# Half passes of q side by side in the two row halves of TensorE, with other first and last stages, in a two-layer decoder kernel

## What is computed

```python
x = _layernorm(x + _L0_attn_ref(x, ...))         # latent attention, 32 heads, causal, rotary
x = _layernorm(x + _L0_xattn_ref(ctx_512, x, ...))  # graph learned from the context, top 30% of a row
x = _layernorm(x + _L0_ffn_ref(x, ...))          # 7 routed experts (best 2) and a shared one
x = _layernorm(x + _L1_attn_ref(x, ...))         # attention, 16 heads, causal, rotary
x = _layernorm(x + _L1_xattn_ref(x, ctx_512, ...))  # bilinear softmax with the context
x = _layernorm(x + _L1_ffn_ref(x, ...))          # gated, 1024 wide
```

## Time and profile before

| | us |
|---|---|
| median of 3 runs | 673.74 (673.16 to 674.34) |
| the profiled execution's own time | 674.2 |
| its span | 672.3 |
| TensorE busy (PE) | 651.7, 97% |
| VectorE busy (DVE) | 524.2, 78% |
| ScalarE busy (ACT) | 502.5, 75% |
| GpSimd busy (POOL) | 389.5, 58% |

### The profile page before, as it was taken

The page is one execution under the profiler, slowest core; times in us unless marked ns, Lnnn a source line. Parts: engine busy times, 40 slices in busy tenths (PEclk is TensorE's granted clock), DMA queues, the critical chain, the costliest instruction groups (busy, mean ns, idle before and its releaser), DMA issues.

```text
span 672.3 us, 15731 instructions
## 1 busy us (share of the span) xinstructions
PE 651.7 (97%) x5342; PEld 557.9 (83%) x5342; DVE 524.2 (78%) x1684; ACT 502.5 (75%) x1305; POOL 389.5 (58%) x646
## 2 busy tenths in 40 slices
PE   8899999999999999999999999999989999999996
PEld 5589988989888899889877888889878887778885
DVE  2799988996999799767889945557798878858455
ACT  4799778878688885898887866665658786876544
POOL 3388658457664845698769455545872321445543
PEclk9999999999999999999999999999999999999998
DMA  8763022214213211310032012111020000011201
GB/s 259 188 186 86 18 71 59 77 26 118 49 56 103 49 50 47 95 33 2 1 96 63 1 54 87 48 49 47 1 95 5 3 3 4 3 48 48 94 1 63
DMA packets 35048, 40.17 MB, mean 60 GB/s; under 512 B 7052, under 2 KB 27798, under 8 KB 34968
## 3 DMA queue, kind: packets, MB, share of 16 engines
q1 hardware_dynamic: 34424, 38.84, 19.8%
q10 hardware_dynamic: 544, 0.33, 0.2%
HBM read 29.05 MB, written 1.05 MB: 45 GB/s over the span
## 4 chain that ended last, share of the span: by engine, by line
PE 82%; DVE 7%; ACT 4%; SPq 2%; issue 2%; DMA 1%; POOL 1%; DVEq 0%; POOLq 0%; ACTq 0%
PE bank L1242 72%; PE bank L1256 8%; SPq L2762 1%; PE bank L1542 1%; ACT probs L1922 1%; DMA xT_plain<-in_xT 1%; POOL qT L2487 1%; DVE bn L2034 1%; DMA qT<-xT_plain 1%; DVE ctx_pair_lo L2011 1%; DVE y L2011 1%; DVE probs L2162 1%; DVE g_pair_lo L2011 0%; ACT x L1684 0%; ACT xT_hi L1677 0%
## 5 line engine op out<-in xcount | busy, mean ns | idle before, releaser
L2484 POOL TENSOR_SCALAR probs<-probs,soft 128x256 f32<-128x256 f32 (+1 forms) x256 | 104.9, 432 | 52.1 <-DVE soft L2170 51.0
L1784 ACT ACTIVATE probs<-probs,soft 128x256 f32<-128x256 f32 (+1 forms) x256 | 113.2, 448 | 12.0 <-DVE soft L2162 11.1
L2487 POOL TENSOR_TENSOR w_split_lo<-w_raw,w_split_hi 128x512 fp32r<-128x512 f32 (+2 forms) x57 | 74.3, 1311 | 67.9 <-ACT w_split_hi L1677 67.7
L1242 PE MATMUL bank<-xT_hi,w_split_hi 128*128 128x512 f32 x256 | 103.8, 405 | 3.7 <-DVE xT_lo L2014 2.5
L1242 PE MATMUL bank<-xT_lo,w_split_hi 128*128 128x512 f32 x256 | 100.5, 393 | 0.0
L1242 PE MATMUL bank<-keyT,qT 128*64 128x192 f32 (+3 forms) x1024 | 80.4, 302 | 1.3 <-POOL qT L2487 1.3
L1242 PEld LDWEIGHTS bank<-keyT,qT 128*64 128x64 f32 x1024 | 74.2, 137 | 8.9 <-issue 3.6
L1242 PE MATMUL bank<-xT_hi,w_split_lo 128*128 128x512 f32 x192 | 75.5, 393 | 0.0
L2487 POOL TENSOR_TENSOR qT<-qT,xT_plain 64x512 f32<-64x512 f32 x44 | 56.5, 1283 | 31.8 <-DMA qT<-xT_plain 29.7
L2162 DVE CUSTOM_DVE_ANT_0 probs<-bank,mask 128x128 f32<-128x128 f32 (+1 forms) x192 | 58.0, 330 | 17.2 <-PE bank L1242 16.2
L1677 ACT ACTIVATE probsT<-bank 128x384 f32<-128x384 f32 x128 | 53.6, 494 | 13.9 <-PE bank L1256 13.4
(11 more groups left out here) (259 smaller groups left out, 1820.6 us busy)
## 6 DMA issues: line engine op xcount, KB each, us to landing
qT<-xT_plain SPq DMA_DIRECT2D x88, 64.0 KB, 2.0
w_raw_heads<-in_w_o SPq DMA_DIRECT2D x8, 512.0 KB, 4.6
w_raw<-in_w_nopeT SPq DMA_DIRECT2D x8, 384.0 KB, 3.1
qT<-rope_buf SPq DMA_DIRECT2D x40, 64.0 KB, 2.0
...
```

The costliest lines, as they stand in the source:

```text
L1242: return t.matmul(out, lhsT, rhs, start=start, stop=stop, skip_group_check=shared)
L1784: ins = s.activation(p[:, at], p[:, at], ACT.Exp, bias=st[:, 0, r:r + 1], scale=-1.0, accum_out=st[:, 1, r:r + 1])
L2484: return g_.tensor_scalar(out, in0, s1, s2, op0, op1)
L2487: return g_.tensor_tensor(out, in0, in1, op)
```

## The change

1. **q.** A step `q_full n g p` does the eight passes of 128 rows (for each kind the three of the first chunk and rest.hi x qaT.hi), and `q n g p` the two last passes, qaT.lo with the rest's high part, with 64 rows each. The rotary kind's high part stays in rows 0 to 63 and the latent kind's moves to rows 64 to 127 (`rest_rows`), so the two passes lie in different row halves and write two banks. qaT.lo has no zero rows any more. Both banks become ready with `q`; between `q_full` and `q` other steps may stand.
2. **First stage.** `down 1` follows `down 0`, keys are a step of their own (`key_T`, `key_scale`), adj_w, adj_qk, w_v 0 and adj_sim 0 stand ahead of the first q; w_v_latT and w_o of group 0 are loaded between xT0 and xT1, the inputs of w_k 0 behind xT1. ScalarE computes a square root of a constant at its start.
3. **Router.** Tokens are on the rows, the 8 + 8 columns are the high and low parts of the router's weights; VectorE adds the two parts and the bias. The copy and the transpose are gone.
4. **Experts.** u_pair.lo is formed from bank + bias - high part, and the bank is free after VectorE.
5. **out1.** Both bias passes first.
6. **Last stage.** `f_end i` keeps m = 7; m = 4 to 6 are `f_mid 0` (two tiles), `f_mid 1` and `f_mid 2` (one each). The last tile's store is issued by ScalarE.
7. **Order and costs.** A new PE_ORDER and ASIDE; Plan's cost of a shape change is stated per shape that is left (LEAVE) instead of 0.13 for all. `v1 0` moves ahead of `qkv 1 0` and of the first transposes of the second attention.

```diff
-            elif name == "q":
+            elif name == "q_full":
                 n, g, p = k
...
                 for kind in (1, 0):
                     out = wait_bank(("q", n, g, p, ("lat", "rot")[kind]))[:, :]
                     first, rest = (w_q[:, c, kind, 2 * p:2 * p + 2, :] for c in range(2))
-                    mm3(out, first, qaT[:, 0, at], True, False)
-                    mm(out, rest.hi, qaT.hi[:, 1, at], False, False)
-                    mm(out, rest.hi, qaT.lo[:, 1, at], False, True).then_inc(q_ready.sem, 1)
+                    mm3(out, first, qaT[:, 0, at], True, False, True)
+                    mm(out, rest.hi, qaT.hi[:, 1, at], False, False, True)
+            elif name == "q":
+                n, g, p = k
+                rest, at = group_q(g).hi[:, 1, :, 2 * p:2 * p + 2, :], slice(n * HALF, (n + 1) * HALF)
+                for kind in (1, 0):
+                    rows = rest_rows(kind)
+                    mm(bank_of(("q", n, g, p, ("lat", "rot")[kind]))[:, :], rest[rows, kind, :, :], qaT.lo[rows, 1, at],
+                       False, True, True).then_inc(q_ready.sem, 1)
...
+    def rest_rows(kind, low=False):
+
+        return slice(QREST, P) if (kind == 1) != low else slice(0, QREST)
...
-LOADS_AFTER = [("xT0", "xT1"), ("xT1", "xT2")] + [("xT2", name) for name in (
+LOADS_AFTER = [("xT0", "xT1"), ("xT1", 0), ("xT1", "xT2")] + [("xT2", name) for name in (
...
+                    w.wait_ge(*zeroed["unit"])
+                    s.activation(last_root[:, 0:1], plain(ones1[:, 0:1]), ACT.Sqrt)
...
-                terms = [(c, plain(part)) for c in range(DC) for part in (xT_pair.hi, xT_pair.lo)]
-                for n, (c, xt) in enumerate(terms):
-                    for i, tile in enumerate(tiles_of[h]):
-                        ins = mm(out[32 * i:32 * i + NE, 0:P], w_router[:, c, :], xt[:, c, tile * P:(tile + 1) * P],
-                                 n == 0, n == len(terms) - 1, True)
+                terms = [(part, c) for c in range(DC) for part in (xT_pair.hi, xT_pair.lo)]
+                for i, tile in enumerate(tiles_of[h]):
+                    for n, (part, c) in enumerate(terms):
+                        ins = mm(out[:, i * 2 * NE:(i + 1) * 2 * NE], part[:, c, tile * P:(tile + 1) * P],
+                                 w_router_parts[:, c, :, :], i == 0 and n == 0, n == len(terms) - 1, True)
...
-                    tt(up.lo[:, i, :], probs[in_probs.place["e_u", e, h, i]][:, :], plain(up.hi[:, i, :]),
-                       ALU.subtract).then_inc(e_u_lo.sem, 1)
+                    stt(up.lo[:, i, :], bank_of(("e_u", e, h, i))[:, :], b_up[:, e, i:i + 1], plain(up.hi[:, i, :]),
+                        ALU.add, ALU.subtract).then_inc(e_u_lo.sem, 1)
...
-            "e_u": lambda: e_u_copied[tuple(k)], "e_gate": lambda: e_silu[tuple(k)],
+            "e_u": lambda: e_u_lo[tuple(k)], "e_gate": lambda: e_silu[tuple(k)],
...
-f_up 1 7, f_end 0, f_end 1""")
+f_up 1 3, f_down 0 7, f_down 1 1, f_up 1 5, f_down 1 2, f_up 1 6, f_down 1 3, f_up 1 7, f_mid 0, f_mid 2, f_end 0,
+f_mid 1, f_end 1""")
...
+        b, i = LAST_STORED
+        w.wait_ge(*last_normed[b, i])
+        s.dma_start(out_dram[b, i * P:(i + 1) * P, :], x[:, TB * b + i, :]).then_inc(stored[b], 16)
```

More of the change, by code:

```diff
@@ L169 @@
 PE_ORDER = steps_of("""
-down 0, w_k 0, down 1, w_q 0, down_T 0, w_v 1, w_k 1, q 0 0 0, down_T 1, w_q 1, adj_w, w_v 0, adj_qk, q 0 0 1,
-q 1 0 0, s 0 0 0, s 1 0 0, q 1 0 1, adj_sim 0, s 0 0 1, s 1 0 1, q 1 1 0, pT 0 0 0, q 1 1 1, pT 0 0 1, pT 1 0 0,
-pT 1 0 1, s 2 0 0, pv 1 0, pv 0 0, s 2 0 1, w_k 2, s 3 0 1, s 3 0 0, q 0 1 0, out 1 0, pT 2 0 0, out 0 0, pT 2 0 1,
-s 2 1 1, pT 3 0 0, s 2 1 0, q 0 1 1, pT 3 0 1, pv 2 0, s 3 1 0, pv 3 0, s 3 1 1, out 2 0, out 3 0, pT 2 1 0,
-pT 3 1 0, pT 2 1 1, s 0 1 1, s 0 1 0, w_q 2, pT 3 1 1, pv 2 1, s 1 1 0, pv 3 1, s 1 1 1, q 1 2 0, q 1 2 1, pT 1 1 0,
@@ L431, in make_plan @@
         if n < U_EXPERT:
-            stage(("load", n, 0), "SP 2.6, DMA 2.5, WAY 2", *needs)
+            stage(("load", n, 0), "SP 2.6, DMA 2.5, WAY 2", *needs,
+                  *[By(("load", first), "SP") for first, then in LOADS_AFTER if n == then])
             stage(("load", n, 1), "SP 1.15, DMA 2.0, WAY 2", *[("w_v", n - 2)] if n >= 2 else [])
@@ L449, in make_plan @@
-        stage(("down_T", h), "PE 1.4, ACT 1.65, DVE 1.35", ("down_scale", h), ("down_rope", h), ("load", "identity"),
-              holds=[bank("qaT", h, c, left=(("down_T", h), "DVE")) for c in range(2)]
-              + [bank("keyT", h, left=(("down_T", h), "ACT"))], items=3)
-        stage(("key_swap", h), "SP 1.2, DMA 0.8, WAY 2", By(("down_T", h), "ACT"))
+        stage(("down_scale", h), "POOL 1.25, ACT 1.4", ("down_root", h), ("load", "const"), items=4)
+        stage(("key_scale", h), "DVE 0.95", ("down_root", h), ("load", "const"))
@@ L454, in make_plan @@
+        stage(("down_T", h), "PE 0.9, ACT 1.1, DVE 1.35", ("down_scale", h), ("load", "identity"),
+              holds=[bank("qaT", h, c, left=(("down_T", h), "DVE")) for c in range(2)], items=2)
+        stage(("key_T", h), "PE 0.45, ACT 0.55", ("key_scale", h), ("down_rope", h), ("load", "identity"),
+              holds=[bank("keyT", h, left=(("key_T", h), "ACT"))])
+        stage(("key_swap", h), "SP 1.2, DMA 0.8, WAY 2", By(("key_T", h), "ACT"))
     for g in range(NG):
         before = [] if g < 2 else [s for part in unit_readers(g - 2) for s in part]
-        stage(("w_k", g), "PE:cols64 0.7, ACT 0.85", ("load", g, 0),
+        stage(("w_k", g), "PE:cols64 0.65, ACT 0.65", ("load", g, 0),
@@ L538, in make_plan @@
         for h in range(NHALF):
-            stage(("e_u", e, h), "PE 2.79, ACT 2.5, DVE 1.3", ("split", U_EXPERT + e, 0), *[("xT", "experts", b) for b in halves(h)],
-                  *MOE_ROOM_LEFT, holds=[bank("e_u", e, h, i, left=(("e_u", e, h), "ACT")) for i in range(DC)]
+            stage(("e_u", e, h), "PE 2.79, ACT 2.5, DVE 1.4", ("split", U_EXPERT + e, 0), *[("xT", "experts", b) for b in halves(h)],
+                  *MOE_ROOM_LEFT, holds=[bank("e_u", e, h, i, left=(("e_u", e, h), "DVE")) for i in range(DC)]
                   + [Hold("probs", ("e_u", e, h, i), By(("e_gate", e, h), "POOL")) for i in range(DC)]
@@ L887, in write_program @@
     xT_hi = signal("xT_hi", keys("xT"))
-    route_copied = signal("route_copied", keys("route_lin"))
     route_exp = signal("route_exp", keys("route_soft"))
@@ L1606, in tensor_program @@
                 for i in range(TB):
+                    mm(out[:, i * D:(i + 1) * D], ones1[:, :], bias1[:, 3 * D:], i == 0, False, True)
+                for i in range(TB):
                     part = out[:, i * D:(i + 1) * D]
-                    mm(part, ones1[:, :], bias1[:, 3 * D:], i == 0, False, True)
                     for c in range(DC):
```

277 lines of the change are left out of this document (151 added, 126 removed), and 4 rows, old and new, of the table ASIDE.

## The result

The changed kernel takes **679.92 us** (median of 7 runs, 676.97 to 682.03), before 673.87 on the same chip (7 runs, 673.16 to 675.02): a ratio of 1.0082, 95% interval 1.0064 to 1.0099. It is slower by 0.82%, where 0.4% faster was forecast and 675.2 was the end of the range. The profiled execution took 679.6, its span is 677.7, so 5.4 us more than the 672.3 before. One of the twelve executions of run 8 took 2234 us and is left out of what is said of it.

The account below looks back on a forecast made before the run. TensorE was taken as the bound, busy 651.7 of 672.3 us; +0.8 (half passes), -2.7 (start), -1.0 (second attention), -0.2 (router), 0 (experts) and +0.2 (tail) gave -2.9, so median 670.8 us, range 666.0 to 675.2.

Parts of the forecast that it names:

- The start, "I take -2.7": Before 40 us: moved work fills TensorE's hole ahead of q and a wait for x goes; -2.7 us, between -3.7 and 0.
- the readiness that the prediction priced at 0: First attention: q's rotary bank is released 1.2 us later, ahead of scores; cost 0, up to +1.5 if cover fails.
- rival (c): First scores wait for q's later rotary part as long as TensorE waited before, giving back the start's gain; 673.4 us, chance 0.18.
- Half passes, +0.8: q steps: paired half passes gain 7.3 us, 61 more shape changes cost 8.1; net +0.8, ends -1.8 and +4.0.
- the 0.053 us a change: Shape changes on TensorE: alternative estimate from a 128-cycle drain, 3.3 us for 61, net -4.0; not adopted.
- Router, -0.2: Router: sixteen narrow passes replace sixteen groups, and a copy and transpose with a 0.39 wait go; -0.2 us, between 0 and -0.5.
- Second attention, -1.0: Start of the second attention: v1 0 moved ahead covers TensorE's 0.87 wait and part of 1.47; -1.0 us, between 0 and -1.8.
- Experts, 0: Experts: reading bank and bias saves DVE 4 us, but TensorE hardly idles there; worth 0, +0.5 at worst.
- Tail, +0.2: Last stage: f_mid 2 ahead of f_end 0 delays the last y, ScalarE's store saves about 0.4; +0.2 us, between -0.5 and +1.
- Rival (d): q's pairs dearer: second half pass 0.10 late, each shape change 0.12 instead of 0.09; 675.8 us, chance 0.17.
- The lower end of the range: Whole kernel: 666.0 us, from a further 3.1 us of idle gaps closed (667.7, chance 0.15) with the half passes' better end.

Follow-up runs that it names:

- run 8: The kernel before with one edit in SP's queue: the loads of group 2 put ahead of the key swap and the swap of q 0 0 0; 675.24 us, 1.0017.
- run 5: The changed kernel with one edit in SP's queue: the swaps of q 0 0 0 put ahead of the loads of group 2; 681.04 us, 1.0086.
- Run 2: The kernel before with q's last two passes behind the eight others, all ten over 128 rows, so only the order is changed; 673.31 us, 0.9976.
- run 1: The kernel before with only q's last two passes made half passes side by side, behind the eight full ones; 676.47 us, 1.0029.
- run 9: The kernel before with only the experts' low part formed from bank, bias and high part, the bank free after VectorE; ratio 1.0006.
- run 3: The changed kernel with q's two last passes over all 128 rows, same place in the order; 680.08 us, 1.0082.
- run 10: The kernel before with only v1 0 moved ahead of qkv 1 0; ratio 1.0024.

## Why the prediction was wrong, by its own steps

**The start, "I take -2.7", is the step that failed.** That 2.6 us of work would fill the hole of 2.5 ahead of q 0 0 0 was right: the wait there is gone, and adj_w, adj_qk, w_v 0 and adj_sim 0 were done by 24.5. The waits came to +1.7 all the same, by two omissions.

One is ahead of the hole. The first down pass before, and both down steps now:

```profile
6.45 2.40 PE L1242 MATMUL bank<-w_down,xT_plain 128*128 128x320 f32 x8 [0.56 <-DMA w_down<-in_L_attn_kv_a_w]
```

```profile
7.24 4.55 PE L1260 MATMUL bank<-w_down,xT_plain 128*128 128x320 f32 x16 [1.34 <-DMA w_down<-in_L_attn_kv_a_w]
13.16 4.57 PE L1260 MATMUL bank<-w_down,xT_plain 128*128 128x320 f32 x16 [1.37 <-DMA xT_plain<-in_xT]
```

The prediction names 1.4 us in which TensorE idles for the last load of x, and its -2.7 leaves them out: measured 1.37. The first down pass waits 1.34 us for its weights where it was 0.56. That isn't chance: in the seven traces of the changed order this wait is 0.75 to 1.50, in the seven of the old one 0.17 to 0.68. The 640 KB that now go ahead of the second piece of x are the likely reason; no run tests them. The first q starts at 25.45, before at 24.75.

The other is behind the hole: I didn't ask what the first scores wait for. The trace of before, which I had, says it. GpSimd's row and the last full pass ahead of the scores:

```profile
32.98 2.66 POOL L2487 TENSOR_TENSOR qT<-qT,xT_plain 64x512 f32<-64x512 f32 x2 [8.64 <-DMA qT<-xT_plain]
...
35.93 0.40 PE L1242 MATMUL bank<-xT_lo,w_split_hi 128*128 128x512 f32 x1
36.26 2.40 PE L1242 MATMUL bank<-keyT,qT 128*64 128x192 f32 x32
```

The rotary part is there at 35.64, TensorE asks for it at 36.26. The slack was 0.6 us, so unless q itself starts earlier at most 0.6 of the 2.7 could be kept, whatever stood ahead of it. And the change made this chain longer: GpSimd starts on it at 36.03 instead of 32.98. Of these 3.05 us 1.9 are there when VectorE reads the rotary bank (28.03 instead of 26.17), 0.7 because q is later and the rest because the bank ends with the pair, the readiness that the prediction priced at 0; 1.2 more come in SP's queue, where the swap goes out at 31.97 instead of 28.86, now behind the loads of group 2 (runs 5 and 8). Run 2, which has the late bank alone, agrees: its first q starts at 23.6, 1.1 us earlier, its first scores at 35.96, only 0.3 earlier, after a wait of 0.76. I had named this as rival (c) with 0.18, but priced it at the loss of the gain only: "as long there as it did before". I counted the loads moved in front of x on SP's queue, and never listed what is in front of the swaps.

**The clock behind the wait wasn't in the sum.** The kernel before waits 2.50 us at the same place of its life without a fall in its profile, and I took the clock as given. In the changed kernel the wait of 2.31 us is followed by the fall. It belongs to single executions: run 1 has it behind a wait of 2.1, run 9 behind 2.5, run 8 has none behind 2.5 and 2.65. But the changed kernel has more of it: the mean granted clock of its seven executions is 0.992 to 0.996, 0.994 on average, and that of the 74 executions of the kernel before that stood beside the runs 0.994 to 0.999, 0.997 on average. Over 677 us that is a difference of some 1.9 us.

**Half passes, +0.8: near the +0.6 that remains, by luck.** That remainder holds the 1.5 us gained at down_T 0; without them it is about +2.1. That pairs run at once, that the second half pass starts with the first, and that changes eat the gain were right. The isolated pair was under-priced, 0.40 for its two changes against 0.28, perhaps because I read the exit behind masks of 128 columns, where part of it may be hidden in the step that I compared with; this isn't shown. Over a whole kernel a change costs 0.17 to 0.19 (runs 1 to 3), where 8.1 / 61 = 0.13 was taken. And 61 changes were put down to the pairs, of which 27 come with the new order even without half passes (run 3's listing has 169, before 142). In the old order the pairs alone cost 2.2 to 3.2 (runs 1, 2), in the new one they gain about 1. The page "TensorEngine Tiling (Array Packing)" of the Trainium skill, section "Tiling Modes", says that a change of mode drains the engine, and the cost of every change here agrees with it; the 0.053 us a change that I estimated from the 128 cycles on the Trainium skill's page "TensorE: Matmul & The Clock Gate", section "Step-by-step: what each phase is for", is a quarter of the 0.20 measured beside an isolated pair.

**Router, -0.2: wrong, +0.9.** The router's rows in the changed kernel:

```profile
342.86 0.25 PE L1260 MATMUL bank<-w_router_parts,xT_hi 128*128 128x16 f32 x1 [0.21 <-DVE xT_lo L2043]
342.96 0.26 PE L1260 MATMUL bank<-w_router_parts,xT_lo 128*128 128x16 f32 x1
343.07 0.26 PE L1260 MATMUL bank<-w_router_parts,xT_hi 128*128 128x16 f32 x1
...
344.52 0.26 PE L1260 MATMUL bank<-w_router_parts,xT_lo 128*128 128x16 f32 x1
344.63 0.47 PE L1260 MATMUL bank<-xT_hi,w_split_hi 128*128 128x512 f32 x1
```

Sixteen passes of 16 columns come every 0.11 us, nearly the 0.12 of passes of 256 columns: 1.77 us from 342.86 to 344.63. Each has a weight load of 128 columns of its own, and these come at the same pace (PEld at 342.93, 343.04 and 343.15). Before, matmuls of 8 stationary columns ran side by side, 32 of them within 1.06 us, and with the wait of 0.39 and the transpose the next pass stood at 339.86, 1.53 us after the first; the second router step took 0.99 and now 1.70. Together that is 0.24 + 0.71, less the transpose of the second step. "Sixteen narrow ones against sixteen groups" should have been priced by a row.

**Second attention, -1.0:** -1.3 measured, inside the range, but not by v1 0 alone (run 10).

**Experts, 0:** right for this part (run 9), though in the changed kernel as a whole TensorE waits 1.10 us there for g_pair_lo, for a reason that no run shows. The mean fell to 749 ns, not to 690, because 690 was the price of a plain subtraction. The six slow instructions of before (861 to 1780 ns) all began while a GpSimd tensor_tensor on probs or w_raw was running, and with one SBUF input less none is slow; that agrees with the Trainium skill's page "SBUF — State Buffer", section "Who interferes with whom", which says that a DVE instruction with two SBUF inputs contends with a GpSimd instruction that reads SBUF.

**Tail, +0.2:** +0.6. The 0.6 later y came as worked out; the 0.4 from the store by ScalarE did not: 0.1.

Rival (d), the pairs dearer and 675.8, had the right sign; its 8.1 + 1.8 + 3.2 over 61 changes is 0.21 us each, near the 0.17 to 0.19 of the runs, but the start is the larger part of the miss. The lower end of the range isn't its own sum: 667.7 less 2.6 is 665.1, not 666.0.
